# Gated cross-attention block: ScalarE instead of SyncE issues x's load and the store of a finished pair

## What is computed

```python
x = x + tanh(g_xattn[0]) * attention(values=ctx, keys=ctx, query=layernorm(x), mask, Wq, Wk, Wv, Wo, biases)   # 16 heads of 16
x = x + tanh(g_ffn[0]) * tanh(layernorm(x) @ W1 @ W2 @ W3 + bias)
```

## Time and profile before

| | |
|---|---|
| median of 3 runs | 1084.88 us (1084.82 to 1089.64) |
| profiled execution | 1076.65 us, span 1074.9 us |
| TensorE busy | 1021.6 us, 95% |
| VectorE busy | 953.5 us, 89% |
| ScalarE busy | 829.0 us, 77% |
| GpSimd busy | 803.6 us, 75% |
| packets of SyncE's queue | 51.6% of 16 DMA engines' time |
| HBM traffic | 144 GB/s over the span |

### The profile page before, as it was taken

One profiled execution on the slowest core, in us unless ns is written; L12 is line 12 of the kernel. 1 busy time (PEld: TensorE's weight loads), 2 busy tenths in 40 slices (PEclk: granted clock), 3 DMA queues, 4 the chain that ended last, 5 costly groups with the idle time before them and its releaser, 6 DMA issues.

```text
span 1074.9 us, 45461 instructions
## 1 busy us (share of the span) xinstructions
PE 1021.6 (95%) x18487; PEld 891.9 (83%) x18487; DVE 953.5 (89%) x1331; ACT 829.0 (77%) x1275; POOL 803.6 (75%) x1184
## 2 busy tenths in 40 slices
PE   5988999999999999999999999999999999999974
PEld 4777888888888888788888888888888888888864
DVE  4778999999999999899999999899989999899866
ACT  4466888887788888788888788788878887878842
POOL 5245888777888887787888887788777787888753
PEclk9999999999999999999999999999999999999989
DMA  5134555655555555565565555555556556555432
GB/s 155 45 100 110 157 154 159 165 146 158 162 161 157 154 165 145 144 177 143 158 169 148 164 151 164 149 150 164 155 144 174 148 159 165 151 162 142 127 114 97
DMA packets 260401, 158.88 MB, mean 148 GB/s; under 512 B 174945, under 2 KB 227170, under 8 KB 260194
## 3 DMA queue, kind: packets, MB, share of 16 engines
q1 hardware_dynamic: 260050, 155.72, 51.6%
q10 hardware_dynamic: 144, 0.26, 0.1%
HBM read 85.92 MB, written 68.94 MB: 144 GB/s over the span
## 4 chain that ended last, share of the span: by engine, by line
PE 46%; SPq 19%; DMA 16%; issue 7%; POOL 5%; DVE 5%; ACT 0%; POOLq 0%; DVEq 0%
PE ps_m L500 9%; PE ps_m L507 9%; DMA scratch_y<-yn 8%; PE ps_s L636 8%; PE ps_s L615 7%; PE ps_x L647 6%; SPq L215 5%; PE ps_m L574 4%; DMA scratch_m<-max_T 4%; SPq L303 4%; DMA q_aug<-scratch_m 3%; SPq L292 3%; PE ps_s L621 2%; SPq L206 2%; DVE probs L1021 2%
## 5 line engine op out<-in xcount | busy, mean ns | idle before, releaser
L1010 DVE TENSOR_REDUCE neg_max<-ps_s 128x16 f32<-128x2048 f32 x128 | 291.4, 2277 | 45.2 <-PE ps_s L621 44.7
L1021 DVE TENSOR_TENSOR probs<-ps_s,far_T 128x2048 f32<-128x2048 f32 x128 | 293.2, 2291 | 34.0 <-PE ps_s L636 33.8
L810 ACT ACTIVATE probs<-probs 128x2048 f32<-128x2048 f32 x128 | 245.0, 1914 | 6.3 <-DVE probs L1021 6.0
L785 ACT ACTIVATE q_aug<-ps_m,q_bias,q_scale 128x256 f32<-128x256 f32 x256 | 123.5, 563 | 58.0 <-PE ps_m L500 49.4
L615 PE MATMUL ps_s<-k_aug,q_aug 32*128 32x128 f32 x4096 | 150.8, 283 | 15.7 <-DVE probs L1021 8.8
L636 PE MATMUL ps_s<-q_aug,k_aug 32*128 32x128 f32 x4096 | 152.2, 284 | 9.7 <-DMA q_aug<-scratch_m 6.6
L615 PEld LDWEIGHTS ps_s<-k_aug,q_aug 32*128 32x128 f32 x4096 | 128.2, 186 | 36.5 <-issue 28.3
L636 PEld LDWEIGHTS ps_s<-q_aug,k_aug 32*128 32x128 f32 x4096 | 128.2, 187 | 28.2 <-DMA q_aug<-scratch_m 9.9
L647 PE MATMUL ps_x<-probs,v_ones 128*32 128x128 f32 x4096 | 140.4, 278 | 3.5 <-issue 2.7
L785 ACT ACTIVATE k_aug<-ps_m,k_bias,parity 128x256 f32<-128x256 f32 x256 | 123.6, 563 | 19.5 <-PE ps_m L500 19.5
L429 POOL TENSOR_TENSOR aT<-a_norm,aT 128x512 fp32r<-128x512 f32 x61 | 78.3, 1284 | 78.3 <-ACT aT L760 78.3
(11 more groups left out here) (123 smaller groups left out, 1731.3 us busy)
## 6 DMA issues: line engine op xcount, KB each, us to landing
scratch_a<-a_den SPq DMA_DIRECT2D x64, 512.0 KB, 3.5
x_in<-in_x SPq DMA_DIRECT2D x64, 256.0 KB, 4.3
a_rows<-scratch_a SPq DMA_DIRECT2D x64, 256.0 KB
den_wide<-scratch_r SPq DMA_DIRECT2D x64, 256.0 KB
out<-y SPq DMA_DIRECT2D x64, 256.0 KB, 4.8
ctx_in<-in_ctx SPq DMA_DIRECT2D x252, 64.0 KB, 2.7
scratch_y<-yn SPq DMA_DIRECT2D x59, 256.0 KB, 4.5
y_blocks<-scratch_y SPq DMA_DIRECT2D x236, 64.0 KB, 2.4
```

The lines of the kernel that those rows point to most:

```text
L785: last = nc.scalar.activation(dst[:, :, 2 * m + a, :], src[:, m * TOK:(m + 1) * TOK].rearrange("p (n q) -> p n q", q=P), ACT.Identity, bia ...
L810: nc.scalar.activation(tile, tile, ACT.Exp).then_inc(probs_ready, 1)
L1010: nc.vector.tensor_reduce(neg_max[:, 0:H].rearrange("p (j c) -> p j c", j=G), ps_s[:], AX.X, ALU.max, negate=True).then_inc(max_ready, 1)
L1021: nc.vector.tensor_tensor(probs[i % 2][:].rearrange("p j s q -> p (j s) q"), ps_s[:].rearrange("p j s q -> p (j s) q"), far_T[:].unsqueeze ...
```

## The change

In every turn of the loop `store(t-7)` and `load_x(t+4)` are taken out of SyncE's order. ScalarE issues them, the load first, after the copy of v and ahead of tanh. Each keeps its wait, now on ScalarE. The loads of x's first four pairs and the last seven stores stay on SyncE.

```diff
--- before.py
+++ after.py
@@ -311,8 +311,6 @@
             load_first()
             load_later()
             for t in range(NP):
-                if is_pair(t - 7):
-                    store(t - 7)
                 if is_pair(t - 5):
                     read_y(t - 5)
                 write_max(2 * t)
@@ -321,8 +319,6 @@
                 read_max(2 * t)
                 if is_pair(t - 2):
                     write_a(t - 2)
-                if is_pair(t + 4):
-                    load_x(t + 4)
                 if is_pair(t + 3):
                     load_ctx(t + 3)
                 write_max(2 * t + 1)
@@ -834,6 +830,14 @@
 
                 nc.scalar.dma_start(dst[:], src.rearrange("(p k) n -> p k n", k=KT)).then_inc(landed, 16)
 
+            def load_x(p):
+                wait(act, y_ready, p - X_RING + 1)
+                nc.scalar.dma_start(x_in[p % X_RING][:], x_v[:, p]).then_inc(x_landed[p % X_RING], 16)
+
+            def store(p):
+                act.wait_ge(res_ready, p + 1)
+                nc.scalar.dma_start(out_v[:, p], y[p % Y_RING][:]).then_inc(y_stored[p % Y_RING], 16)
+
             def split(dst, src, landed):
                 act.wait_ge(landed, 16)
                 nc.scalar.activation(flat(dst[:, 0]), flat(src[:]), ACT.Copy).then_inc(w_high, 1)
@@ -859,6 +863,10 @@
                     keep_a(2 * t - 3)
                 if t >= Q_EARLY:
                     keep_v(t)
+                if is_pair(t + 4):
+                    load_x(t + 4)
+                if is_pair(t - 7):
+                    store(t - 7)
                 if is_pair(t - 6):
                     tanh(t - 6)
                     gate(t - 6)
```

## The result

The changed kernel takes 1106.78 us in the median of 4 runs (1103.2 to 1112.09), the kernel before 1084.91. The ratio is 1.0216, with a 95% interval of 1.0157 to 1.0276: slower by 2.2%, where 0.7% faster was forecast. A second comparison gave 1.0235 (1.0175 to 1.0295). The profiled execution took 1109.71 us, with a span of 1107.9.

What follows compares the result with a forecast made beforehand. TensorE was taken as nearly always busy, with SyncE's lateness costing 11.6 us in the steady part. Terms: -8.0 (SyncE) + 0 (ScalarE, GpSimd) + 0.3 (start) = -7.7, so 1084.9 became 1077 us; range 1066 to 1095.

Steps and rivals of the forecast that it cites:

- What bounds the kernel: Steady loop: TensorE busy 889.1 of 900 us; relieving SyncE, late at write_y, can bring at most 11.6 us.
- The floor of 15.63 us: Period of an undisturbed turn; 56 such turns would take 875.6 us, where the profile had 887.2.
- What the change takes from SyncE: SyncE's queue up to write_y: x's load leaving saves 8.0 us, bounds 0 and 11.6; the store's going counts nothing.
- What it puts on ScalarE: Two issues ahead of tanh: tanh starts 0.97 us later, bounds 0.86 and 2.0, at cost 0.
- The threshold on the way through finish, the root and xn: Path from tanh through GpSimd to TensorE: TensorE stalls only from a tanh delay of 1.18 us.
- The bound of 2.0 us: Upper bound of tanh's delay on ScalarE, with one issue as long as SyncE's 1.53 us load.
- the first rival: Issues on ScalarE are dearer, for instance through a shared descriptor generator: 1091 us, or 1116 if both wait; chance 0.22.
- Places where no row has the answer: DMA engines: x's load and the store's packets at new times, unpriced by any row, taken as 0.
- The third rival: X's load and the store collide with y_blocks and the maxima's round trip: +11 - 8, 1088 us; chance 0.08.
- The start: Before the steady loop: load_x(4) issued while x's fourth load is in flight, +0.3 us, 0 to 1.
- No relief: SyncE's queue: stalls come from a full queue and fall on ctx instead, so 1082 us; chance 0.22.
- no effect: ScalarE could sit in load_x's wait where y comes late; gives the forecast's time, no separate chance.

Runs made afterwards that it cites:

- the copy of 1.92 us: Kernel before plus a 128x2048-element copy on ScalarE, behind the wait for y and ahead of tanh, no DMA moved: 1107.68 us, ratio 1.0196.
- the run with the load later: Against the kernel before, ScalarE issues the store ahead of tanh without a y wait, x's load behind the even batch's copy of a: 1073.2 us, ratio 0.9869.
- the store alone at the late place: Against the kernel before, only the store goes to ScalarE, ahead of tanh but held behind the wait for y_ready: 1094.64 us, ratio 1.0072.

## Why the prediction was wrong

**What bounds the kernel.** Right. The floor of 15.63 us was there in the undisturbed turns of every kernel but the one with the copy of 1.92 us, and the 11.6 us above it were mostly SyncE's lateness: the run with the load later took 8.7 us of them away, where the sum had 8.0.

**What the change takes from SyncE.** The 8.0 us were right for a load that leaves SyncE and goes to a harmless time. For the change as made they never came, because SyncE lost at `read_max` what it had gained, and more: it waited 66.6 us for the maxima's write there, against 14.2, and was late with `write_y` in 32 turns against 15. (Its order has 23 DMAs a turn, not 22; nothing hangs on it.) The store's going was counted at nothing and, issued ahead of y, was worth nothing (0.9987).

**What it puts on ScalarE.** The term for an issue, 0.465 us, was too high for the load (0.375) and about right for the store's median (0.486). Tanh was 0.93 us late in the median turn, where 0.97 had been worked out. The threshold on the way through finish, the root and xn was right to 0.01 us. What failed is the step from one price to all turns: the store stands directly behind a 256 KB load in the same queue, and its issue reached 2.18 us. The bound of 2.0 us had been written down for just that, from SyncE's stalled load, and then left out of the value. It costs about 6.9 us, measured by moving it behind the gating. This was a part of the first rival, but not by its mechanism, a shared generator: with SyncE's issues beside it the load's issue never took over 0.445 us.

**"Places where no row has the answer".** This is the step that lost the forecast. It took 0 for x's load moving from 4.7 to 0.8 us after the add, and 0 for the store's later packets, "since the engines' share of 0.56 leaves room". (The store's issue moved further than the 2 to 3 us written down: from 2.2 us before the first y_blocks issue to 1.7 us behind it, 3.9 us.) The runs show in its place +0.6% for the load alone, +0.7% for the store alone at the late place, and +1.7% for both with no stall in front of tanh. A share averaged over 900 us said nothing on the two microseconds in which the even maxima make their round trip: there it rose from 0.50 to 0.74, while the average fell from 0.56 to 0.54. The third rival named the mechanism and got 0.08. Its price, 0.2 us per turn, was too small as well: the turns outside the 11 with a stalled store lie 28.9 us above the floor (37.5 less 8.6) instead of 11.6, so 17.3 us more, where the rival had 11 less 8, so 3 us more. Its argument against, that the store's packets are on the engines then anyway, didn't hold: the run with the late store shows that 2.2 us later is another matter.

**The start.** 0.3 us were taken and at most 1; the profile shows 3.6. VectorE's statistics of x's fourth pair come 1.5 us later (25.04 against 23.58). Whether the 3.6 us come from this is not settled: in the run with the load later VectorE waits only 3.23 us for that pair, less than the 4.10 of the kernel before, and yet the second add comes at 107.77 us, the latest of all. TensorE's granted clock from 25 to 50 us was 0.80 in both, instead of 0.93.

**No relief and no effect, the other rivals.** Not what happened: SyncE was relieved once x's load went to a harmless time, as the later load shows, and ScalarE's wait for y held nothing up by itself.

## What to carry to other kernels

A DMA that is moved has a time of flight that moves with it: look up which small transfer with a waiting reader is under way at the new moment, and don't take an average share of the DMA engines as room. A wait put into an engine's order moves everything queued behind it, so of two issues that look alike, the one that has nothing to wait for should go first, and the one with the wait last: here the swap alone is worth 1.7%. The slack behind an engine can be read from idle times along the path closely, here 1.18 us against 1.17 measured, but the delay that is held against it must be the longest, not the median.

## What was not expected of the hardware

An issue of x's load took 0.375 us as the median on ScalarE's queue, in the loop of the kernel before 0.47 on SyncE's. That need not be the engine: SyncE's own last five stores, behind the loop, took 0.37 to 0.38 us each. A second one directly behind it took 0.49 as the median and up to 2.18, while the same store with nothing ahead of it in its queue took 0.39 and at most 0.44. A 16 KB write that took 2.19 us from its issue to the read behind it took 3.0 to 3.1 with 256 KB of x under way, alike from either queue, although the 16 DMA engines were busy only 0.76 to 0.80 of the 2 us behind its issue.
